# A four-part graph network on one core: GAT picks begun in the node stage, and the update passes' head products and edge-product copy moved

## What is computed

```python
L0:  att = sigmoid([x[head], rel[type]] @ att_w + att_b);  tanh(segment_sum(att * x[tail], head) @ W.T + b)
L1:  five GAT layers (four standard with gelu, one "skip" on [in_x, x]):
       h = x @ W; logit = leaky_relu(h @ a_src [src] + h @ a_dst [dst]); alpha = segment_softmax(logit, dst)
       out = segment_sum(alpha * h[src], dst) + b
L2:  dot attention: e = leaky_relu(sum(k[src] * q[dst])); softmax over dst; sum of f[src] * a
L3:  three passes, i = 0..2, 4 heads:
       scores = (q[dst] . k[src]) / 4 + e @ We[i];  softmax over dst;  h = LN(h + agg @ Wo[i])
       e = LN(e + gelu([h_old[src], h_old[dst], e] @ Wem[i] + bem[i]))       (edge features, 32 wide)
```

## Time and profile before

| | |
|---|---|
| median of 3 runs | 10914.1 us (10911.99 to 10914.28) |
| the profiled execution | 10918.62 us, its span 10916.8 us |
| busy, share of the span | POOL 73%, DVE 60%, PE 48%, ACT 43% |
| five gat passes, POOL's gathers | 588 each, about 737 us each |
| dot and multi passes | 784 gathers each |

### The profile page before, as it was taken

One profiled execution on the slowest core, in us unless ns is written; L12 is line 12 of the kernel. 1 busy time (PEld: TensorE's weight loads), 2 busy tenths in 40 slices (PEclk: granted clock), 3 DMA queues, 4 the chain that ended last, 5 costly groups with the idle time before them and its releaser, 6 DMA issues. The chain is left out here.

```text
span 10916.8 us, 87549 instructions
## 1 busy us (share of the span) xinstructions
PE 5191.6 (48%) x22037; PEld 4373.7 (40%) x22037; DVE 6547.4 (60%) x11572; ACT 4657.7 (43%) x5207; POOL 8001.4 (73%) x7864
## 2 busy tenths in 40 slices
PE   5344426885885786688588400011111433343333
PEld 5333425774774676577477300011111322232222
DVE  6333325664665566566466555554555688858887
ACT  0010004664664665566466322223333455535553
POOL 7888885776776776777677677767776777757774
PEclk8555556996997898799699655555555566656665
DMA  5333333332332232233254333333443555535553
GB/s 191 34 34 38 34 21 87 81 82 49 83 79 64 67 81 72 58 81 82 62 135 129 103 113 120 121 92 126 133 131 110 162 176 183 176 116 177 184 175 103
DMA packets 693316, 1131.52 MB, mean 104 GB/s; under 512 B 403255, under 2 KB 468070, under 8 KB 685558
## 3 DMA queue, kind: packets, MB, share of 16 engines
q0 software_dynamic: 364224, 383.74, 18.7%
q1 hardware_dynamic: 265088, 397.86, 11.4%
q10 hardware_dynamic: 63926, 349.09, 8.1%
HBM read 674.29 MB, written 468.68 MB: 105 GB/s over the span
## 5 line engine op out<-in xcount | busy, mean ns | idle before, releaser
L877 POOL DMA_INDIRECT turned<-d_t,idx x6076 | 5749.1, 946 | 1921.6 <-issue 1851.3
L1032 PE MATMUL banks<-pair,hot 128*128 128x462 f32 x13720 | 3177.7, 395 | 680.0 <-DVE wide L1127 586.0
L1032 PEld LDWEIGHTS banks<-pair,hot 128*128 128x128 f32 x13720 | 2759.3, 203 | 1097.5 <-DVE wide L1127 678.3
L648 POOL DMA_INDIRECT d_acc<-work,idx x784 | 1237.9, 1579 | 252.0 <-issue 234.4
L1237 DVE COPY idx<-src 128x28 int32 x252 | 45.8, 182 | 1871.5 <-DMA turned<-d_t,idx 1868.8
L1325 DVE TENSOR_TENSOR_SCAN wide<-banks,wide 128x224 f32<-128x224 f32 (+1 forms) x1008 | 1023.7, 1077 | 6.0 <-DVE wide L1319 0.3
L930 ACT ACTIVATE hot<-wide,row 128x896 fp32r<-128x896 f32 x980 | 930.1, 1030 | 77.7 <-DMA wide<-d_key 48.9
L1064 PE MATMUL banks<-ident,wide 128*128 128x128 f32 x588 | 162.0, 421 | 1681.3 <-ACT wide L897 863.2
L1305 DVE TENSOR_TENSOR wide<-turned,banks 128x1792 f32<-128x1792 f32 x252 | 860.3, 3414 | 0.0
L1003 ACT COPY wide<-wide 128x924 f32<-128x924 f32 (+1 forms) x252 | 477.2, 1894 | 873.2 <-DVE wide L1325 869.3
L1064 PEld LDWEIGHTS banks<-ident,wide 128*128 128x128 f32 x588 | 102.3, 211 | 1748.8 <-ACT wide L897 894.4
(11 more groups left out here) (295 smaller groups left out, 8308.5 us busy)
## 6 DMA issues: line engine op xcount, KB each, us to landing
d_e<-wide ACTq DMA_DIRECT2D x168, 924.0 KB
turned<-d_t,idx POOLq DMA_INDIRECT x6076
d_e<-wide ACTq DMA_DIRECT2D x84, 1008.0 KB
wide<-d_b SPq DMA_DIRECT2D x60, 1344.0 KB
wide<-d_key SPq DMA_DIRECT2D x145, 448.0 KB, 3.7
wide<-d_b SPq DMA_DIRECT2D x60, 896.0 KB, 4.6
d_b<-wide SPq DMA_DIRECT2D x28, 1344.0 KB
wide<-d_edge SPq DMA_DIRECT2D x84, 448.0 KB, 5.3
```

The source lines that it names most:

```text
L648: gp.indirect_dma_start(g.d_acc[r][:, :], offset(idx[:, b, k:k + 1]), sums[:, b, k, :], None, compute_op=ALU.add).then_inc(added[b][r], 16)
L877: gp.indirect_dma_start(rows[:, b, k, :], None, table[:, :], offset(idx[:, b, k:k + 1])).then_inc(s["gathered"][b], 16)
L1032: mm = nc.tensor.matmul(ps_cols[i], hot[:, place, i, j, :], flat(g.pair[:, part, j]), start=(j, part) == (0, 0), stop=(j, part) == (SETS - ...
```

## The change

1. **Picks.** AHEAD becomes 2. A class `Picks` holds the signals, keys, membership and one-hots. It is made before the node stage, which now loads the first keys, makes the first one-hots on ACT (at its start in gat stages, at its end in the sum stage) and splits the table set by set on DVE (`split(j)`, in gat stages behind `finish(j+1)`). The four gat passes behind a gat node stage get `ahead=2`: 14 more columns of chunk 0 are picked, POOL gathers 7 columns of chunk 0 instead of 21, and step n serves chunk n-3. The first pass has `ahead=0`. DVE takes the first steps before it waits for the seed.
2. **Sum stage.** SP's load of group j no longer stands behind the store of the group before it, but two groups ahead of the stores.
3. **Update passes.** `spread_q(2)` and `product_q(1)`, `product_q(2)` move: only head 1's product stands inside the layer norm, and heads 2 and 3 come behind it.
4. **Multi passes.** `save_product` is divided. `copy_logits` comes behind `widen_mask`, and the copy and store of the edge product behind the exponentials.
5. Some scratch tiles move; `tmp` of the node stage is two columns wider and serves the split as well.

```diff
-AHEAD = 0
+AHEAD = 2
@@ edges, SP
-        for n in range(1, AHEAD + 4 if X else 1):
-            if n > 1:
-                sp.wait_ge(s["hot_made"], n - 1)
-            sp.dma_start(keys, step_keys(n)).then_inc(s["keys_loaded"], 16)
+        for n in range(2, AH + 4 if X else 2):
+            sp.wait_ge(picks["hot_made"], n - 1)
+            sp.dma_start(keys, step_keys(g, X, n + AT)).then_inc(picks["keys_loaded"], 16)
@@ edges, POOL
-            gather(0, 0, KG - X * AHEAD)
+            gather(0, 0, KG - X * AH)
             gather(0, 1, KG)
@@ edges, ACT
-            if multi:
-                save_product(chunk, cols)
             if wide_rows:
                 act.wait_ge(s["q_done"], chunk + 1)
                 widen_mask((chunk + 1) * K)
+            if multi:
+                copy_logits(chunk)
             if X and more:
-                one_hots(chunk + 3, 1 - b)
+                one_hots(nc, g, act, pk, chunk + AH + 3, (b + AH + 1) % 2)
             act.wait_ge(s["logits_done"], chunk + 1)
             nc.scalar.activation(weights, factors[:, 1], ACT.Exp)
...
             wide.then_inc(s["factors_wide"], 1)
+            if multi:
+                save_product(chunk, cols)
@@ edges, DVE
-        if X:
-            v.wait_ge(ready["result_copied"], ready["copied"])
-            split_table()
-        v.wait_ge(ready["spread_done"], 16 * C)
-        v.wait_ge(ready["seeded"], 16)
+        if not X:
+            v.wait_ge(ready["spread_done"], 16 * C)
+            v.wait_ge(ready["seeded"], 16)
...
+        if X:
+            link = Link(v, s["first_link"])
+            for n in range(1, AH + 1):
+                at = KG - X * (AH + 1 - n)
+                take(n, 0, at, 0, EARLY, link)
+                take(n, 0, at, EARLY, X, link)
+            take(AH + 1, 0, KG, 0, EARLY, link)
+            v.wait_ge(ready["spread_done"], 16 * C)
+            v.wait_ge(ready["seeded"], 16)
...
         if X:
-            link = Link(v, s["first_link"])
-            take(1, 0, 0, EARLY, link)
-            take(1, 0, EARLY, X, link)
+            take(AH + 1, 0, KG, EARLY, X, link)
@@ edges, DVE, an update chunk
                 link(product_q(G, 0))
                 link(spread_q(b, 1))
-                link(product_q(G, 1))
-                link(spread_q(b, 2))
                 v.wait_ge(s["gelu_done"], chunk + 1)
...
-                link(product_q(G, 2))
+                link(product_q(G, 1))
...
-                for i in range(0 if not update else 3, NH):
+                for i in range(0 if not update else 2, NH):
@@ nodes, SP
+        if pk is not None:
+            load_first_keys(nc, g, sp, pk)
+        if summing:
+            for j in range(BUFS, NG):
+                sp.wait_ge(s["summed"], j - BUFS + 1)
+                load_sums(j)
+                if j > BUFS:
+                    store_tables(j - BUFS - 1)
+        for j in range(NG - BUFS - 1 if summing else 0, NG if out_w else 0):
+            store_tables(j)
@@ nodes, DVE
+        def split(j):
+            v.wait_ge(s["result_copied"], NB * (j + 1))
+            split_set(nc, g, v, pk, j, heads)
...
             if not mix and j + 1 < NG:
                 finish(j + 1)
+            if pk is not None and not summing:
+                split(j)
@@ nodes, ACT (a second call stands at the end of the sum stage)
+        if pk is not None and not summing:
+            first_hots()
```

More of the change, by code:

```diff
@@ L212, in start @@
         g.key = ph.sbuf("key", [P, KT])
+        g.ones = ph.sbuf("ones", [P, P])
+        g.before, g.after = ph.sbuf("before", [P, P]), ph.sbuf("after", [P, P])
         ph.now = ph.block(drained=False)
@@ L696, in widen_maxima, with edges @@
     return nc.vector.tensor_copy(out[:, width:width + heads], maxima)
-def edges(nc, g, ph, banks, rows, tiles, ready, kind, a=None, update=False, clear=None):
+def edges(nc, g, ph, banks, rows, tiles, ready, kind, pk=None, a=None, update=False, clear=None, ahead=0):
     H = NH if kind == "multi" else 1
@@ L767, in edges @@
     if X:
[L768 to L771, removed]
+        picks, keys, hot, member, found = pk.s, pk.keys[:], pk.hot, pk.member, tiles["found"]
+        AH, AT = pk.ahead, pk.first
         ps_cols = [banks[:, i % RING, 0:SET * TW] for i in range(X)]
@@ L921, in turn_b @@
             nc.scalar.copy(b_f[:, b], b_rows[:].rearrange("p k f -> p f k")).then_inc(s["b_turned"], 1)
[L924 to L928, removed]
[L929 to L940 removed]
         act.dma_start(prime[0:1, 0:1], g.d_x[0:1, 0:1]).then_inc(s["stored"], 16)
[L943 to L946 removed]
+        for n in range(2, AH + 3 if X else 2):
+            one_hots(nc, g, act, pk, n, n % 2, n == 2)
+            one_hots_end(nc, act, pk, n, n % 2)
         for b in range(2):
@@ L1309, in one @@
             if X and (more or b == 0):
-                take(chunk + 2, 1 - b, 0, EARLY, link)
+                take(chunk + AH + 2, 1 - b, KG, 0, EARLY, link)
             if update:
@@ L1420, in nodes @@
     agg_T, rows_T = turned["agg_T"], turned["rows_T"]
-    agg, part, st, own, tmp = (tiles[n] for n in "agg part st own tmp".split())
+    agg, part, st, own, heads = (tiles[n] for n in "agg part st own tmp".split())
+    tmp = heads[:, :, 0:D]
     wide = ph.sbuf("wide", [P, FZ])
@@ L1587, in _ @@
                 finish(j + 1)
+            if pk is not None and not summing:
+                split(j)
+        if pk is not None and summing:
+            for j in range(NG):
+                split(j)
     def turned_rows(step, j):
@@ L1713, in layer @@
         ph.now = ph.block()
-        ready = nodes(nc, g, ph, banks, turned, wide, **node)
+        pk = Picks(nc, ph, edge["kind"], edge["ahead"]) if edge and edge["kind"] in COLS else None
+        ready = nodes(nc, g, ph, banks, turned, wide, pk=pk, **node)
         if edge:
-            edges(nc, g, ph, banks, rows, chunk, ready, **edge)
+            edges(nc, g, ph, banks, rows, chunk, ready, pk=pk, **edge)
 class Graph:
```

141 lines of the change are left out of this document (77 added, 64 removed).

## The result

| | median, us | runs |
|---|---|---|
| before | 10913.05 (10910.63 to 10914.28) | 4 |
| changed | 10753.1 (10747.28 to 10753.24) | 4 |

The account below looks back on a forecast made before the run. Bounds: POOL's gather count in gat passes, DVE's cycle in update passes, late loads in the sum stage. Terms 70 + 29.5 + 76 - 1 = 174.5 us off 10914.1 gave 10740 us, range 10715 to 10795.

Parts of the forecast that it names:

- Picks: Four gat passes lose 14 gathers each in chunk 0, with no new wait of POOL: -70 us, bounds 0 and 70.
- rival of late picks: Chunk 0 of the gat passes: late picks stall POOL beyond 21.6 us of slack, total 10775 to 10810 us; chance 0.06.
- low clock: PE's picks: clock stays at the lower level, 36.8 us a step; ten such steps a pass give 11160 us; chance 0.03.
- Node stages: Node stages before the four gat passes: first keys may delay the first state's fetch, +1 us; earlier split counted as nothing.
- Sum stage: Loads of partial sums issued a group earlier should be there when DVE needs them: -29.5 us, bounds 15 and 34.8.
- Update passes: Two idle gaps of DVE close in each chunk, its cycle falls from 36.43 to 34.7 us: -76 us for both passes.
- 28.3: Update passes: POOL's waits for DVE, less the normal 0.30 us between gathers, go away: 28.3 us a pass.
- 8.6 for the lag: End of an update pass: DVE's lag at the last chunk falls from 10.6 to about 2 us, saving 8.6.
- 1.7 for the chunk: End of an update pass: DVE's last chunk is 1.7 us shorter, within POOL's 53.3 us wait there.
- The forecast's own test: Update passes: DVE's chunks 35.0 us apart if right; 35.3 or more would mean DVE still sets the pace.
- Update passes give half: Rival: the moved pieces are not the limit, ACT's state copies are; term 40 to 48 us, total 10770; chance 0.12.
- Late loads: Rival: sum-stage loads stay late as groups share DMA queues; term 10 to 15 us, total 10758; chance 0.07.

## Why the prediction was right, and where it was off

**Picks: right, -75.1 for -70.** POOL meets no new wait, and the passes lose what 14 gathers cost. In the run of this part alone the same pass took 719.80 us, 17.9 less than before, or 71.6 for four; the rest of the 75.1 is within what two executions differ. The timing inside it was too careful. PE was to start at 2637.6; in fact it was well into its picks by then:

```profile
2614.82 35.37 PE L1067 MATMUL banks<-pair,hot 128*128 128x462 f32 x168
```

I had let PE wait for the last set's split "as now"; it works from the first set on. The rival of late picks did not occur, nor that of a low clock (granted 0.95 over the pass).

**Node stages: the step that failed, +13.2 for +1.** Its two sentences were "The first keys ... may delay that by some tenths: +1 for the four" and "I count nothing for it: the same seven sets stand beside POOL's DMAs before and after, only earlier". The keys cost 5.2 us (POOL's wait 1.0 to 1.8 longer in each stage). The second sentence was wrong in its reason. A DMA of POOL is lengthened when it begins inside the subtraction with about half of it or more still to run: all that began 0.25 to 0.52 us behind the start of one were, and those that began in its last 0.03 us were not. Before, the seven sets ran back to back and fell into step with the scatters: one scatter starts at 2638.24, before the second subtraction, and the next at 2639.50, as it ends (2638.52 + 0.98). So 13 DMAs over 1.1 us began in one, 9 began in its last moment, the sum stage included. Spread over the stage, 23 do, and 11 of 1.11 to 1.17 us begin in the bitwise operation where one did. With the scratch in PSUM the 13.2 us came off; together with late keys, 19.3. I had seen the row of 1.42 us and priced it by counting instructions instead of DMAs that would meet them.

The Trainium skill ("SBUF — State Buffer", SBUF: two separate sides) explains such rows by descriptors that GpSimd can't write while VectorE holds the shared port, and gives a copy from SBUF to SBUF as the case. The traces agree in that a DMA ends a fixed time behind the instruction that it began in: 2563.47 + 0.99 = 2564.46, and 2563.74 + 1.42 = 2565.16, 0.70 us behind, and those that began 0.2 us later end at the same distance. They differ in the instruction: the split's cast from SBUF to SBUF held none, and the bitwise operation and the TENSOR_TENSOR with both inputs in SBUF did. That it is the port is not shown by any run here; shown is that moving the scratch to PSUM ends it. By the whole 2.6 us of a set, as I had weighed it, the term would have been 73 us; by the 13.2 us that came off, a set costs some 0.5.

**Sum stage: right, -31.6 (alone -29.3) for -29.5.** The first six roots are 10.1 to 10.8 us apart, the last 9.4 behind, and no load is late.

**Update passes: -68.1 for -76.** "28.3" of POOL's waits held: the pass lost 27.9. The exponentials' wait of 0.3 us and, with the products alone, the gelu's of 1.04 held too. The mis-sized terms are the two at the pass's end, 8.6 for the lag and 1.7 for the chunk: the idle time behind the pass fell by 6.1 us (53.3 to 47.2) and not by 10.3, so 4.2 for each pass, 8 for both. Of the 6.1 us, 4.7 are DVE's smaller lag behind the last gather (10.6 to 5.9) and the other 1.4 the shorter last chunk. "DVE's lag of 10.6 us at the last chunk falls to about 2" was taken from the first chunk. Its last gather and DVE's first instruction, and the same at the end of the pass:

```profile
8480.79 0.94 POOL L926 DMA_INDIRECT turned<-d_t,idx  x1 [0.30 <-issue]
...
8483.44 0.18 DVE L1268 COPY idx<-src 128x28 int32 x1 [13.12 <-DMA turned<-d_t,idx]
...
9427.88 0.94 POOL L926 DMA_INDIRECT turned<-d_t,idx  x1 [0.30 <-issue]
...
9434.74 0.17 DVE L1268 COPY idx<-src 128x28 int32 x1
```

At the start the gather lands 1.7 us behind its end (8481.73 to 8483.44); in the middle of the pass, at 185 GB/s, it took 4.8 us. So DVE's lag ends at 5.9 us (9428.82 to 9434.74). DVE does not wait in this last chunk, so if the gather lands after 4.8 us here too, 1.1 us of the lag are DVE's own. The forecast's own test, "35.3 us apart or more would mean that it still sets the pace", was met from below with 35.23. The waits for gathers decide it: POOL sets the pace. The chunks that don't meet the gathers run at 34.1 to 35.0 us from norm to norm (8981.31 - 8946.47 = 34.84; 9015.39 - 8981.31 = 34.08), near the forecast's 34.7; those that do take 36.1 to 36.6.

The drain of "ScalarE: Activation LUTs", What ACT_TABLE_LOAD costs, in the Trainium skill would by the prediction's estimate have left about 0.9 us of wait for the exponentials. The rows show 0.3, so no drain is to be seen in the changed kernel either.

**The rivals.** "Update passes give half" is out: half of DVE's saving alone gives 70 to 75% of the gain (47.5 and 51.2 of 68). Late loads, late picks and the low clock did not occur on this chip. A slower outcome did on the other: there the picks alone cost 53 us, with PE pausing between matmuls. The mean granted clock was 0.64 there, against 0.70 in the run of the same kernel that gained 60.6 us; what part the clock has in it was not looked at.

**The total.** Between the profiled executions the gain is 9 us short of the forecast (165.8 for 174.5): 20 us in the two misses, less 11 in rows that came out larger than forecast. Most of those 11 are the pace of the execution of the kernel before, so that the total came this near is in part luck.

## What to carry to other kernels

Where two engines share a ring of buffers, a saving in the slower one pays until its cycle is a little above the faster one's: with 27 rounds and 8 us of slack, 0.3 us over is free. So the second of two such savings is worth less than the first. When work is moved beside another engine's DMAs, count which of those DMAs it will now meet, not only whether it stood beside some before; and see where its operands lie. Scratch in PSUM took 13 us off four node stages whose computation didn't change.

## What was not expected of the hardware

- A TENSOR_TENSOR of DVE with both inputs in SBUF (128x462, 0.98 us) lengthened an indirect DMA of POOL that began 0.25 to 0.52 us behind its start from 0.95 to 1.18 to 1.47 us, so that it ended 0.7 us behind the instruction. DMAs that began in its last 0.03 us took 0.96 us. A bitwise TENSOR_SCALAR from SBUF to SBUF (0.40 us) did the same to DMAs that began 0.05 to 0.16 us behind its start (1.08 to 1.17 us), and the cast between the two (0.98 us) did it to none of 22. With the scratch in PSUM none was lengthened by the split.
- A load of 448 KB on SP's queue 0.3 us ahead of a small indirect fetch made POOL's wait for what is computed from that fetch 1.0 to 1.8 us longer.
- The same gather lands 1.7 us behind its end on POOL at the start of an update pass and 4.8 us in its middle.
- The kernel before took 10907 to 10913 us in three measurements and 14140 us in a fourth, on another chip. There PE paused 1116 times between independent matmuls, up to 7.9 us, and the profile names no releaser. The mean granted clock was 0.64 there against 0.69, 8% less beside 30% more time.
